# The last projection with w3 stationary and 512 tokens moving; x1 is turned instead of z2

## The chip, the cores and the metric

One core of one Trainium2 chip runs the whole program. The metric is the time of one execution on the device, in microseconds (us). TensorE is PE in the views, VectorE is DVE, ScalarE is ACT, GpSimd is POOL; SP is the engine that issues most DMAs, and its rows are "SPq".

## The reference

The input is 16 sequences of 256 tokens with 256 features. A first block adds to x a gated attention over a context (an mLSTM form with 8 heads), fed with the layer norm of x. A second block is the feed-forward part that this change touches:

```python
x = x + attention(layernorm(x), ctx)                # called x1 in the kernel
h = silu(lin(layernorm(x), w1, s1)) * lin(layernorm(x), w2, s2)   # 256 -> 1024
h = gelu(lin(h, h1, s)); h = gelu(lin(h, h2, s))    # 1024 -> 1024, twice
x = x + lin(h, w3, s3)                              # 1024 -> 256, scaled per output feature
```

The weights of the linear layers are ternary, each with one scale per output feature. layernorm(x1) is called z2.

## The kernel before, in words

The work is cut into 8 pairs of sequences, 512 tokens each. `batch(i, ...)` is written once for each engine and unrolled over i = 0 to 7. In batch i TensorE runs the feed-forward part of pair i, and between its matmuls stand the attention of pair j = i + 1 and the gates of pair g = i + 2. In batches 0 to 5 all three are there, batch 6 has no gates (`g_stage` is false), batch 7 only the feed-forward part.

Feed-forward values are held features by tokens: the partitions are 128 features, the 512 tokens are the free axis. Each value is split into two parts, a rounded `h_hi` (ACT) and the rest `h_lo` (DVE), and each product is two matmuls. A layer has 8 groups m of 128 output features; a group of a hidden layer is 16 matmuls with 512 moving columns. There are four steps in a batch: `swiglu` (64 matmuls), two `hidden_layer`s (128 matmuls each, the second is called layer 3 in the code's `after_3`), and `project`.

After each group of a hidden layer ACT applies the gelu and makes `h_hi` (`gelu`, L762 and L765), and DVE makes `h_lo` (`lo`, L1184). DVE's program is one fixed list: what stands between two `lo` calls delays the later one. `gelu` of group m waits for `lo` of group m - 4, since they share a buffer of four. `project` waits for `lo` of group k before it uses the values of group k, and for all groups' PSUM banks to be free.

The second norm of pair j lies in batch i = j - 1, around layer 3: DVE makes x1 in `xs` (`residual`), its moments (`norm_2_stats`), the inverse root (`norm_rsqrt`, 11 small instructions), and z2, tokens by features (`norm_2_apply`, L906). TensorE turns z2 into features by tokens (`turn_z2`, 8 transposes, L1356) right ahead of `project`; ACT and DVE split it into `z2_hi` and `z2_lo` (L744, L1165), for which the first matmul of the next batch waits (`s_z2lo`).

`project` of before has the hidden values stationary (128 features by 128 tokens) and 256 columns of w3 moving, so its result is tokens by features, like x1; `finish` scales it by w3's scales (L1196) and adds x1 (L1202).

The SP engine's list is in one order as well, and each DMA may wait for a semaphore, with all behind it waiting too. In batch 6 it writes x1 of pair 7 to DRAM (`keep_x1`, L439), and then issues `load_raw` for 10 blocks of the raw weights (L459). They go to `decay`, four slots in turn, and DVE's `compare` (L1235) looks at each block for a weight that the rounding changed. If there were one, a second path over all pairs would run from the x1 kept in DRAM; with these inputs that path is skipped. `compare` of blocks 0 to 5 stands on DVE behind `lo` of groups 2 to 7 of batch 6.

For the first norm of pairs 2 to 7 the kernel has another form already: the input is loaded features by tokens, and mean and inverse root are written to DRAM (`moment_rows`, L379), read back spread over all partitions into `z` (L381), and applied with two `tensor_tensor` operations (`norm_in_place`, L933 and L935).

## Time and profile before

| | |
|---|---|
| median of 3 runs | 759.57 us (757.95 to 759.61) |
| profiled execution | 757.76 us, its span 756.0 us |
| granted TensorE clock | 0.999 over the span |
| busy: PE, DVE, ACT, POOL | 745.9, 540.9, 366.2, 23.9 us |

The span runs from the first to the last instruction. A matmul's shown duration is longer than the distance to the next one's start, since matmuls are pipelined; the distances between starts are what TensorE pays. Times in the rows below are counted from the span's start.

### The profile page before, as it was taken

The numbers are of one execution on the slowest core, as the hardware profiler recorded it, in microseconds if no ns is written. First come the engines' busy times: TensorE is split into PE (matmuls) and PEld (weight loads), VectorE is DVE, ScalarE is ACT, GpSimd is POOL, SyncE is SP. The second block draws the span as 40 slices with busy tenths as digits, with TensorE's granted clock in tenths as the row PEclk, the third lists the DMA queues.
The fourth block names the chain that finished last, engine by engine and source line by source line (L and its number), as shares of the span: only waits on it lengthen the run. The fifth ranks groups of instructions, "written<-read, shape, count | busy, mean of one in ns | idle before, by whom it ended". The sixth has DMA issues, their size and how long they took to land.

```text
span 756.0 us, 15309 instructions
## 1 busy us (share of the span) xinstructions
PE 745.9 (99%) x6344; PEld 620.3 (82%) x6344; DVE 540.9 (72%) x1289; ACT 366.2 (48%) x559; POOL 23.9 (3%) x52
## 2 busy tenths in 40 slices
PE   8999999999999999999999999999999999999998
PEld 4778888888898888988888888888789888898887
DVE  6788686686957859587785869669595774965554
ACT  3566436463535625456364644556253562445332
POOL 3400000000000000000000000000000000000000
PEclk9999999999999999999999999999999999999999
DMA  8293213202022030411232031320202100540540
GB/s 335 83 406 145 62 62 138 84 28 87 34 113 84 29 87 35 151 45 33 86 125 101 1 92 58 113 85 28 87 34 113 56 1 3 194 140 27 168 140 31
DMA packets 19417, 70.38 MB, mean 93 GB/s; under 512 B 4128, under 2 KB 6160, under 8 KB 16528
## 3 DMA queue, kind: packets, MB, share of 16 engines
q1 hardware_dynamic: 17760, 57.03, 22.1%
q0 software_dynamic: 1296, 11.53, 3.9%
q8 instruction: 52, 0.85, 0.5%
q10 hardware_dynamic: 288, 0.79, 0.3%
q14 instruction: 21, 0.17, 0.1%
HBM read 60.42 MB, written 8.92 MB: 92 GB/s over the span
## 4 chain that ended last, share of the span: by engine, by line
PE 93%; DVE 1%; issue 0%; ACT 0%
PE ps_f L1605 31%; PE ps_f L1606 31%; PE ps_f L1570 8%; PE ps_f L1571 8%; PE ps_f L1645 4%; PE ps_f L1646 4%; PE ps_a L1510 2%; PE ps_a L1493 2%; PE ps_a L1543 1%; PE ps_a L1356 1%; PE ps_a L1466 1%; PE ps_a L1502 0%; PE ps_f L1580 0%; DVE stats L1078 0%; DVE z L1065 0%
## 5 line engine op out<-in xcount | busy, mean ns | idle before, releaser
L1605 PE MATMUL ps_f<-h_hi,wgt 128*128 128x512 f32 x1024 | 401.5, 392 | 0.0
L1606 PE MATMUL ps_f<-h_lo,wgt 128*128 128x512 f32 x1024 | 398.8, 389 | 0.0
L1605 PEld LDWEIGHTS ps_f<-h_hi,wgt 128*128 128x128 f32 x1024 | 192.2, 188 | 41.9 <-ACT work L762 1.2
L1606 PEld LDWEIGHTS ps_f<-h_lo,wgt 128*128 128x128 f32 x1024 | 192.3, 188 | 39.2
L762 ACT ACTIVATE work<-ps_f,scl 128x512 f32<-128x512 f32 x128 | 87.7, 686 | 221.3 <-PE ps_f L1606 221.1
L1184 DVE TENSOR_TENSOR h_lo<-work,h_hi 128x512 fp32r<-128x512 f32 x128 | 85.5, 688 | 91.2 <-ACT h_hi L765 90.3
L1570 PE MATMUL ps_f<-h_hi,wgt 128*128 128x512 f32 x252 | 99.2, 393 | 0.0
L1571 PE MATMUL ps_f<-h_lo,wgt 128*128 128x512 f32 x252 | 98.3, 390 | 0.0
L749 ACT ACTIVATE work<-ps_f,scl 128x512 f32<-128x512 f32 x64 | 44.2, 690 | 88.3 <-PE ps_f L1571 87.6
L765 ACT ACTIVATE h_hi<-work 128x512 fp32r<-128x512 f32 x128 | 81.0, 633 | 4.1
L1175 DVE SCALAR_TENSOR_TENSOR work<-ps_f,scl,work 128x512 f32<-128x512 f32 x64 | 48.1, 751 | 39.5 <-PE ps_f L1571 38.3
L1000 DVE SCALAR_TENSOR_TENSOR decay<-decay,cols,future 128x128 f32<-128x128 f32 x224 | 64.5, 364 | 0.0
L1645 PE MATMUL ps_f<-wgt,h_hi 128*128 128x256 f32 x256 | 62.4, 285 | 0.0
L1646 PE MATMUL ps_f<-wgt,h_lo 128*128 128x256 f32 x256 | 61.8, 283 | 0.0
L1570 PEld LDWEIGHTS ps_f<-h_hi,wgt 128*128 128x128 f32 x252 | 47.3, 188 | 10.6 <-DVE work L1175 0.4
L1571 PEld LDWEIGHTS ps_f<-h_lo,wgt 128*128 128x128 f32 x252 | 47.3, 188 | 9.4
L1646 PEld LDWEIGHTS ps_f<-wgt,h_lo 128*128 128x128 f32 x256 | 49.1, 192 | 0.0
L1645 PEld LDWEIGHTS ps_f<-wgt,h_hi 128*128 128x128 f32 x256 | 49.1, 192 | 0.1
L675 ACT ACTIVATE decay<-decay 128x1024 f32<-128x1024 f32 x28 | 29.7, 1061 | 35.3 <-DVE decay L1000 35.3
L1180 DVE TENSOR_TENSOR h_lo<-work,h_hi 128x512 fp32r<-128x512 f32 x64 | 43.7, 682 | 0.8
L753 ACT ACTIVATE h_hi<-work 128x512 fp32r<-128x512 f32 x64 | 39.9, 623 | 4.4 <-DVE work L1175 4.3
L1016 DVE SCALAR_TENSOR_TENSOR decay<-ps_a,decay 128x512 f32<-128x512 f32 x60 | 37.1, 678 | 1.1 <-PE ps_a L1493 1.1
(207 smaller groups left out, 596.2 us busy)
## 6 DMA issues: line engine op xcount, KB each, us to landing
decay<-m_rows SPq DMA_DIRECT2D x14, 1024.0 KB, 6.6
decay<-w_cols SPq DMA_DIRECT2D x22, 512.0 KB, 4.5
wgt<-w_cols POOLq DMA_DIRECT2D x5, 1024.0 KB, 11.6
v_aug<-ctx_tok SPq DMA_DIRECT2D x8, 528.0 KB, 5.0
wgt<-w_cols POOLq DMA_DIRECT2D x2, 2048.0 KB, 13.7
x_kept<-xs SPq DMA_DIRECT2D x8, 512.0 KB, 2.7
xs<-x SPq DMA_DIRECT2D x7, 512.0 KB, 3.6
ctxT<-ctx_t SPq DMA_DIRECT2D x7, 512.0 KB, 3.3
```

The costliest lines, as they stand in the source:

```text
L749: act.activation(work[:, m % 2], ps_f[:, bank], ACT.Silu, scale=scl[:, 0, m:m + 1]).then_inc(s_silu, 1)
L762: act.activation(work[:, m % GELU], ps_f[:, (turn_of(i) + m) % 4], ACT.Gelu, scale=scl[:, 2 + layer, m:m + 1]).then_inc(s_gelu, 1)
L765: act.activation(h_hi[1 - layer][:, m], work[:, m % GELU], ACT.Copy).then_inc(s_hi, 1)
L1000: last = dve.scalar_tensor_tensor(part, part, cols[:, t, row:row + 1], future[:], ALU.subtract, ALU.add)
L1175: dve.scalar_tensor_tensor(work[:, 2 + m % 2], ps_f[:, bank], scl[:, 1, m:m + 1], work[:, m % 2], ALU.mult, ALU.mult).then_inc(s_hf, 1)
L1184: dve.tensor_tensor(h_lo[1 - layer][:, m], work[:, m % GELU], h_hi[1 - layer][:, m].bitcast(F32), ALU.subtract).then_inc(s_lo, 1)
L1570: pe.matmul(ps_f[:, bank + half], w, moving(z2_hi[:, c], as_is), start=(c == 0), stop=False)
L1571: last = pe.matmul(ps_f[:, bank + half], w, moving(z2_lo[:, c], as_is), start=False, stop=(c == CH - 1))
L1605: pe.matmul(ps_f[:, bank], w, moving(h_hi[layer][:, k], as_is), start=(k == 0), stop=False)
L1606: last = pe.matmul(ps_f[:, bank], w, moving(h_lo[layer][:, k], as_is), start=False, stop=(k == KH - 1))
L1645: pe.matmul(to, moving(h_hi[0][:, k, q * P:(q + 1) * P], as_is), w, start=(k == 0), stop=False)
L1646: last = pe.matmul(to, moving(h_lo[0][:, k, q * P:(q + 1) * P], as_is), w, start=False, stop=(k == KH - 1))
```

## The change

- `project` has w3 stationary (128 hidden by 128 output features) and 512 tokens moving: 32 matmuls of 512 columns where 64 of 256 stood. The last pair's second half is cut in two pieces of 256 tokens. The result is features by tokens, so `finish` is one operation for each of two banks, with w3's scale per partition, and the output is written in that layout.
- x1 must be in that layout too. TensorE turns x1 (`turn_x1`) behind group 4 of layer 3, where it turned z2 behind group 7; ACT copies it from PSUM into `xs` (`take_x1T`) behind the gelu of group 4.
- The second norm is done on the turned x1: DVE's `norm_rsqrt` and two small copies of the moments (`keep_moments`) stand ahead of `lo` of group 0; SP sends the moments to DRAM and spreads them back (`spread_moments(1, ...)`); `norm_2_turned`, two `tensor_tensor` of 1024 columns, stands behind `lo` of group 5. `z2_hi` and `z2_lo` are made from SBUF.
- `keep_x1` waits for the turned x1, and z2 is kept in DRAM as well (`keep_z2`, 8 more DMAs of 512 KB). Pair 0 keeps its z2 in an extra ACT copy, and its x1 is turned in `swiglu`, behind m = 3.
- `compare` writes its marks into `zT` instead of `z`.

```diff
-            def spread_moments(j):
-
-                sp.wait_ge(s_moments, j - W + 1)
-                reuse(sp, s_moments_in, 16 * (j - W))
-                sp.dma_start(moment_rows.rearrange("k p q -> p k q"), moments[:]).then_inc(s_moments_out, 16)
-                sp.wait_ge(s_moments_out, 16 * (j - W) + 16)
+            def spread_moments(n, turn):
+
+                rows_out = moment_rows[n]
+                sp.wait_ge(s_moments[n], turn + 1)
+                reuse(sp, s_moments_in[n], 16 * turn)
+                sp.dma_start(rows_out.rearrange("k p q -> p k q"), moments[n][:]).then_inc(s_moments_out[n], 16)
+                sp.wait_ge(s_moments_out[n], 16 * turn + 16)
+                if n:
+                    sp.wait_ge(s_zTe, min(turn + 3, PAIRS))
                 sp.dma_start(z[:].rearrange("p q d -> p (q d)"),
-                             moment_rows.rearrange("(o k) p q -> o (k p q)", o=1).to_broadcast([P, 2 * NT])).then_inc(s_moments_in, 16)
+                             rows_out.rearrange("(o k) p q -> o (k p q)", o=1).to_broadcast([P, 2 * NT])).then_inc(s_moments_in[n], 16)
...
             def keep_x1(j):
-                sp.wait_ge(s_resid, RESIDUAL_STEPS * (j + 1))
-                sp.dma_start(x1_kept[j], xs[j % 2][:]).then_inc(s_x1kept, 16)
+                sp.wait_ge(s_x1T, j + 1)
+                sp.dma_start(x1_kept[j], resident_turned(j)).then_inc(s_x1kept, 16)
+
+            def keep_z2(j):
+                if first(j):
+                    sp.wait_ge(s_z2_taken, 1)
+                else:
+                    sp.wait_ge(s_z2, j)
+                sp.dma_start(z2_kept[j], z2_turned).then_inc(s_z2kept, 16)
...
+            keep_z2(0)
             keep_x1(0)
...
-                    spread_moments(g)
+                    spread_moments(0, g - W)
...
                 if j < PAIRS:
+                    spread_moments(1, j - 1)
                     keep_x1(j)
...
+                if j < PAIRS - 1:
+                    keep_z2(j)
                 if i == PAIRS - 2:
                     for n in range(COMPARED_BEFORE_LAST + RAW):
                         load_raw(n)
+                    keep_z2(j)
...
-                act.wait_ge(s_z2T, j + 1)
-                act.activation(z2_hi, ps_a[:, 0:CH], ACT.Copy).then_inc(s_z2hi, 1)
+                if isinstance(j, int):
+                    act.wait_ge(s_z2, j)
+                else:
+                    act.wait_ge(s_z2in, 16 * (j - PAIRS) + 16)
+                act.activation(z2_hi, z2_turned, ACT.Copy).then_inc(s_z2hi, 1)
+
+            def copy_first_z2():
+
+                act.activation(z2_turned, ps_a[:, 0:CH], ACT.Copy).then_inc(s_z2_taken, 1)
+
+            def take_x1T(j):
+                act.wait_ge(s_x1turn, j + 1)
+                if not first(j):
+
+                    act.wait_ge(s_norm2, NORM_STEPS * (j - 1) + 1)
+                act.activation(resident_turned(j), ps_a[:, 0:CH], ACT.Copy).then_inc(s_x1T, 1)
...
+                    if a_stage and m == 4:
+                        take_x1T(j)
...
+            def norm_2_turned(j):
+                dve.wait_ge(s_moments_in[1], 16 * (j - 1) + 16)
+                dve.wait_ge(s_x1T, j + 1)
+                dve.tensor_tensor(by_tile(z2_turned), by_tile(resident_turned(j)), moment_spread(0), ALU.subtract).then_inc(s_z2_centred, 1)
+                dve.wait_ge(s_z2_centred, j)
+                dve.tensor_tensor(by_tile(z2_turned), by_tile(z2_turned), moment_spread(1), ALU.mult).then_inc(s_z2, 1)
...
             def finish(i):
 
-                kept = resident(i)[:].rearrange("p (b t) d -> p b (t d)", b=W)
-                scale = w3s_b[:].rearrange("p (o d) -> p o d", o=1).to_broadcast([P, TILES, DIM])
+                kept = resident_turned(i)
                 if first(i):
                     dve.wait_ge(s_w3s, 16)
-                for b in range(W):
-                    dve.wait_ge(s_ymm, Q * i + W * TILES - W + b + 1)
-                    bank = (turn_of(i) + b) % 4
-                    dve.tensor_tensor(y_tmp[:, b].rearrange("p (t d) -> p t d", t=TILES),
-                                      ps_f[:, bank].rearrange("p (t d) -> p t d", t=TILES), scale, ALU.mult).then_inc(s_ysc, 1)
                 if isinstance(i, int):
                     dve.wait_ge(s_x1kept, 16 * i + 16)
-                for b in range(W):
-                    dve.wait_ge(s_ysc, W * i + b + 1)
-                    dve.tensor_tensor(kept[:, b], y_tmp[:, b], kept[:, b], ALU.add).then_inc(s_y, 1)
+                else:
+                    dve.wait_ge(s_x1in, 16 * (i - PAIRS) + 16)
+                for c in range(CH):
+                    dve.wait_ge(s_ymm, CH * i + c + 1)
+                    dve.scalar_tensor_tensor(kept[:, c], ps_f[:, (turn_of(i) + c) % 4], w3s[:, c:c + 1], kept[:, c],
+                                             ALU.mult, ALU.add).then_inc(s_y, 1)
...
                     norm_2_stats(j, xs[j % 2])
+                    norm_rsqrt(s_norm2, j)
+                    keep_moments(1, j - 1)
                 for m in range(KH):
                     lo(i, 1, m)
-                    if a_stage and m == 1:
-                        norm_rsqrt(s_norm2, j)
-                        norm_2_apply(j, xs[j % 2])
+                    if a_stage and m == 5:
+                        norm_2_turned(j)
                     if g_stage and m == 1:
...
-            def turn_z2(j):
-                pe.wait_ge(s_z2, j)
-                turn(z2, ps_a[:, 0:CH], s_z2T)
+            def turn_x1(j):
+                pe.wait_ge(s_resid, RESIDUAL_STEPS * (j + 1))
+                if first(j):
+                    pe.wait_ge(s_z2_taken, 1)
+                    pe.wait_ge(s_z2lo, 1)
+                turn(resident(j), ps_a[:, 0:CH], s_x1turn)
...
             def project(i, as_is, final):
                 per = UNIT // DIM
 
-                def part(b, t, ks):
-                    q = b * TILES + t
-
-                    n = q if final else b
-                    bank, col = (turn_of(i) + n) % 4, 0 if final else t * DIM
+                def part(c, n, at, ks):
+
                     for k in ks:
                         if as_is and k % per == 0:
                             pe.wait_ge(*unit_landed(i - PAIRS, UNIT_W3 + k // per))
 
                         pe.wait_ge(s_lo, 2 * KH * i + KH + max(k + 1, 5 + n))
-                        w = columns(UNIT_W3 + k // per, k % per * DIM, DIM, as_is)
-                        to = ps_f[:, bank, col:col + DIM]
-                        pe.matmul(to, moving(h_hi[0][:, k, q * P:(q + 1) * P], as_is), w, start=(k == 0), stop=False)
-                        last = pe.matmul(to, moving(h_lo[0][:, k, q * P:(q + 1) * P], as_is), w, start=False, stop=(k == KH - 1))
+                        w = columns(UNIT_W3 + k // per, k % per * DIM + c * P, P, as_is)
+                        to = ps_f[:, (turn_of(i) + n) % 4, at]
+                        pe.matmul(to, w, moving(h_hi[0][:, k, at], as_is), start=(k == 0), stop=False)
+                        last = pe.matmul(to, w, moving(h_lo[0][:, k, at], as_is), start=False, stop=(k == KH - 1))
                     return last
 
+                whole, left, right = slice(0, NT), slice(0, SEQ), slice(SEQ, NT)
                 if final:
-                    for t in range(TILES):
-                        part(0, t, range(KH - 1))
-                    for t in range(TILES):
-                        part(0, t, range(KH - 1, KH)).then_inc(s_ymm, 1)
+                    part(0, 0, whole, range(KH - 2))
+                    part(1, 1, left, range(KH - 2))
+                    part(0, 0, whole, range(KH - 2, KH)).then_inc(s_ymm, 1)
                     count_inexact()
-                    for t in range(TILES):
-                        part(1, t, range(KH)).then_inc(s_ymm, 1)
+                    part(1, 1, left, range(KH - 2, KH)).then_inc(s_tail_ymm, 1)
+                    part(1, 2, right, range(KH)).then_inc(s_ymm, 1)
                     return
-                for b in range(W):
-                    part(b, 0, range(KH - 1))
-                for b in range(W):
-                    part(b, 0, range(KH - 1, KH)).then_inc(s_ymm, 1)
-                for b in range(W):
-                    part(b, 1, range(KH)).then_inc(s_ymm, 1)
+                for c in range(CH):
+                    part(c, c, whole, range(KH - 2))
+                for c in range(CH):
+                    part(c, c, whole, range(KH - 2, KH)).then_inc(s_ymm, 1)
...
+                    if first(i) and m == 3:
+                        turn_x1(0)
...
-                    if a_stage and m == 7:
-                        turn_z2(j)
+                    if a_stage and m == 4:
+                        turn_x1(j)```

The lists of three engines show where this moves instructions. SP, around batch 6, before; `xs1` holds pair 7's x1, `w_cols` are the raw weights:

```order
L433 DMA decay<-m_rows 128x2048 x2
L443 DMA out<-xs1 128x1024
L399 DMA xs1<-x 128x1024
L439 DMA x1_kept<-xs1 128x1024
L459 DMA decay<-w_cols 128x1024 x10
L443 DMA out<-xs0 128x1024
```

And SP at the same place after the change:

```order
L413 DMA xs1<-x 128x1024
L391 DMA moment_rows1<-moments1 128x2x4
L395 DMA z<-moment_rows1 128x1024
L453 DMA x1_kept<-xs1 128x1024
L481 DMA decay<-w_cols 128x1024 x10
L460 DMA z2_kept<-num 128x1024
L464 DMA out<-xs0 128x1024
```

The ten weight blocks still stand behind the copy of x1, but that copy now stands behind two new DMAs and waits for the turned x1.

DVE in layer 3 of batch 6, before. L1184 is `lo`, L1235 is `compare`; the rows ahead of the piece are `lo` of groups 0 and 1 and the inverse root:

```order
L906 TENSOR_SCALAR num<-xs1,mv,nw 128x256 x4
L1184 TENSOR_TENSOR h_lo0<-work,h_hi0 128x512
L1235 SCALAR_TENSOR_TENSOR z,inexact<-decay,wgt 128x1024
L1184 TENSOR_TENSOR h_lo0<-work,h_hi0 128x512
L1235 SCALAR_TENSOR_TENSOR z,inexact<-decay,wgt 128x1024
L1184 TENSOR_TENSOR h_lo0<-work,h_hi0 128x512
```

DVE at that place after the change, from the end of the inverse root on; L1238 is `lo`, L1280 is `compare`, L993 and L995 are `norm_2_turned`:

```order
L976 COPY moments1<-mv 128x4
L977 COPY moments1<-nw 128x4
L1238 TENSOR_TENSOR h_lo0<-work,h_hi0 128x512 x3
L1280 SCALAR_TENSOR_TENSOR zT,inexact<-decay,wgt 128x1024
L1238 TENSOR_TENSOR h_lo0<-work,h_hi0 128x512
L1280 SCALAR_TENSOR_TENSOR zT,inexact<-decay,wgt 128x1024
L1238 TENSOR_TENSOR h_lo0<-work,h_hi0 128x512
L1280 SCALAR_TENSOR_TENSOR zT,inexact<-decay,wgt 128x1024
L1238 TENSOR_TENSOR h_lo0<-work,h_hi0 128x512
L993 TENSOR_TENSOR num<-xs1,z 128x1024
L995 TENSOR_TENSOR num<-num,z 128x1024
L1280 SCALAR_TENSOR_TENSOR zT,inexact<-decay,wgt 128x1024
```

The norm has moved from a place ahead of the first `compare` to one behind the third, and is two wide operations.

TensorE at the end of layer 3 of batch 6, before, with z2's eight transposes between the layer and the projection:

```order
L1605 MATMUL ps_f<-h_hi1,wgt 128x512
L1606 MATMUL ps_f<-h_lo1,wgt 128x512
L1356 MATMUL ps_a<-ident,num 128x128 x8
L1645 MATMUL ps_f<-wgt,h_hi0 128x256
L1646 MATMUL ps_f<-wgt,h_lo0 128x256
```

And TensorE behind group 4 of the same layer after the change, with x1's transposes among the layer's matmuls:

```order
L1651 MATMUL ps_f<-h_hi1,wgt 128x512
L1652 MATMUL ps_f<-h_lo1,wgt 128x512
L1398 MATMUL ps_a<-ident,xs1 128x128 x8
L1651 MATMUL ps_f<-h_hi1,wgt 128x512
L1652 MATMUL ps_f<-h_lo1,wgt 128x512
```

The transposes have moved three groups forward, and a second change of form inside the layer comes with them.

## Rows read from the trace of the kernel before

**Rows 1.** The page: busy time by engine, and shares of the last chain.

```profile
PE 745.9 (99%) x6344; PEld 620.3 (82%) x6344; DVE 540.9 (72%) x1289; ACT 366.2 (48%) x559; POOL 23.9 (3%) x52
...
PE 93%; DVE 1%; issue 0%; ACT 0%
```

**Rows 2.** Waits of TensorE: who was waited for, us in total, times, longest.

```profile
PE ps_a L1510 <- issue: 1.9, 1, 1.9
```

**Rows 3.** Timeline of TensorE, batch 6, layer end to next batch: start us, us.

```profile
659.52 0.39 PE L1605 MATMUL ps_f<-h_hi,wgt 128*128 128x512 f32 x1
...
663.15 1.03 PE L1356 MATMUL ps_a<-ident,num 128*128 128x128 f32 x8
663.94 0.36 PE L1645 MATMUL ps_f<-wgt,h_hi 128*128 128x256 f32 x1
...
671.69 0.40 PE L1570 MATMUL ps_f<-h_hi,wgt 128*128 128x512 f32 x1
```

**Rows 4.** Timeline of TensorE in batch 1, behind the gates and behind layer 3.

```profile
197.32 0.50 PE L1605 MATMUL ps_f<-h_hi,wgt 128*128 128x512 f32 x1
197.65 0.40 PE L1606 MATMUL ps_f<-h_lo,wgt 128*128 128x512 f32 x1
...
215.59 1.04 PE L1356 MATMUL ps_a<-ident,num 128*128 128x128 f32 x8
```

**Rows 5.** Timeline of DVE, the last instruction of the span.

```profile
752.88 0.42 DVE L1225 TENSOR_TENSOR xs<-num,xs 128x256 f32<-128x256 f32 x1
```

**Rows 6.** Groups of DVE: busy us, mean ns, then idle before.

```profile
L933 DVE TENSOR_TENSOR zT<-zT,z 128x1024 f32<-128x1024 f32 x6 | 12.0, 2000 | 18.5 <-DMA zT<-x_t 18.5
L935 DVE TENSOR_TENSOR zT<-zT,z 128x1024 f32<-128x1024 f32 x6 | 11.9, 1980 | 0.2
L926 DVE COPY moments<-mv 128x4 f32<-128x4 f32 x6 | 1.0, 170 | 0.2
```

**Rows 7.** DMA issues, median us to landing: the moments on their way out.

```profile
moment_rows<-moments SPq DMA_DIRECT2D x6, 4.0 KB, 2.1
```

**Rows 8.** Line L381, the spread of the moments.

```profile
DMA to landing us min/median/max: 3.7/4.0/5.0
```

**Rows 9.** Line L459, the loads of raw weight blocks.

```profile
DMA to landing us min/median/max: 3.5/4.5/6.6
```

**Rows 10.** Timeline of SP in batch 6.

```profile
647.63 0.34 SPq L439 DMA_DIRECT2D x_kept<-xs  x1
648.01 18.91 SPq L459 DMA_DIRECT2D decay<-w_cols  x10
```

**Rows 11.** Timeline of DVE in batch 6, layer 3.

```profile
649.69 1.29 DVE L1184 TENSOR_TENSOR h_lo<-work,h_hi 128x512 fp32r<-128x512 f32 x2
650.90 0.16 DVE L851 TENSOR_SCALAR nw<-nw 128x4 int32<-128x4 int32 x1
...
653.08 1.39 DVE L906 TENSOR_SCALAR num<-xs,mv,nw 128x256 f32<-128x256 f32 x4
...
655.11 1.22 DVE L1235 SCALAR_TENSOR_TENSOR z<-decay,wgt 128x1024 bf16<-128x1024 f32 x1
...
656.86 1.22 DVE L1235 SCALAR_TENSOR_TENSOR z<-decay,wgt 128x1024 bf16<-128x1024 f32 x1
...
666.49 1.22 DVE L1165 TENSOR_TENSOR h_lo<-ps_a,h_hi 128x1024 fp32r<-128x1024 f32 x1
```

**Rows 12.** Timeline of ACT in batch 6: gelu of group 4, and z2_hi.

```profile
652.47 0.69 ACT L762 ACTIVATE work<-ps_f,scl 128x512 f32<-128x512 f32 x1 [2.27 <-PE ps_f L1606]
...
664.61 1.01 ACT L744 ACTIVATE h_hi<-ps_a 128x1024 fp32r<-128x1024 f32 x1
```

**Rows 13.** Timeline of DVE in batch 1: lo of groups 0 and 1, and 7.

```profile
203.82 1.29 DVE L1184 TENSOR_TENSOR h_lo<-work,h_hi 128x512 fp32r<-128x512 f32 x2
...
217.18 0.69 DVE L1184 TENSOR_TENSOR h_lo<-work,h_hi 128x512 fp32r<-128x512 f32 x1 [2.63 <-ACT h_hi L765]
```

**Rows 14.** A stretch: us, busy of PE, PEld, DVE, ACT, POOL, clock, DMA share, GB/s.

```profile
528.00:536.00 8.00, 6.13 (x180) 5.01 (x179) 6.80 (x27) 3.16 (x5) 0.00 (x0) 1.00 0.03 3
```

143 lines of the change are left out of this document (75 added, 68 removed).

## The prediction

> **What bounds the kernel now.** I read the page first: TensorE is busy in 99% of the span and carries 93% of the chain that ended last, where DVE is busy in 72% and ACT in 48% [rows 1]. In the waits of TensorE one entry has more than a microsecond, 1.9 us once, released by nothing that the profile shows [rows 2]. So the time is the sum of what TensorE issues, and everything else costs only once it is late for TensorE. Then the timeline, for distances between starts: group 7 of layer 3 of batch 6 has 16 matmuls of 512 columns from 659.52 to 663.15, 0.227 us each; the turn of z2 takes 0.79 (663.15 to 663.94), and the 64 matmuls of 256 columns of the projection 7.75 (663.94 to 671.69), 0.121 each [rows 3]. Behind a change of form the first distance is longer: 0.33 where 0.227 is usual, behind the gates [rows 4], and I count 0.1 for it.
>
> **TensorE's own sum.** The projection becomes 32 matmuls of 512 columns: 32 x 0.227 = 7.26, with the first's 0.1 it is 7.4 against 7.75 [rows 3]. That is 0.4 less for each of pairs 0 to 6, 2.8 in all. The last pair has 16 wide and 32 narrow matmuls, 3.63 + 3.87 + 0.1 = 7.6, so 0.15 less. Together -2.95. The columns are the same; what is saved is a fixed part of each matmul (2 x 0.121 - 0.227 = 0.015 us).
>
> x1's turn costs what z2's did, but it stands alone among matmuls of another form, and in batches 0 to 5 the turn of the gate rows then stands alone too. Each such place costs a second first distance, 0.1, and perhaps as much again on entry: I take 0.15 for six batches, +0.9 (bounds 0 and 0.2 each). Pair 0 gets a turn that it did not have: 0.79 + 0.1 [rows 3, 4], so +0.9, with its ACT copies (1.0 each, as the copy of z2 [rows 12]) beside a SwiGLU in which ACT idles. At the end DVE's separate add of 0.42 [rows 5] is gone, since scale and add are one operation: -0.4. The sum of these is -2.95 + 0.9 + 0.9 - 0.4 = about -1.5 us.
>
> At the projection a rule speaks against this term. The Trainium skill, "TensorE: Matmul & The Clock Gate", Back-to-back issue gap, gives an isolated distance of N / 2.4 + 2.5 ns. By it 64 of 256 columns are 6.99 us and 32 of 512 are 6.91, a gain of 0.08 per pair, and as estimates from that page TensorE's sum would be +0.8 instead of -1.5. The rows have a fixed part six times as large, and the sum above goes by them.
>
> **DVE in the batches with gates (0 to 5).** Ahead of `lo` of group 0 now stand the inverse root, 653.08 - 650.90 = 2.2 [rows 11], and two copies (0.17 each, overlapping [rows 6]); counted 0.2. In batch 1 that puts the moments at 203.82 + 2.4 = 206.2 [rows 13]. The trip out takes 2.1 [rows 7] and with the issue I count 2.6; the spread takes 4.0 [rows 8]; so they are back at 212.8. DVE gets to that place at about the same time, since gelu of group 4 and the ACT copy of x1 stand before `lo` of group 5. `norm_2_turned` is of the form of L933 and L935, 2.00 + 1.98 [rows 6], not two of the 1.22 that a plain operation over 1024 columns takes [rows 11]: done at 216.8. `lo` of groups 6 and 7 follow by 218 (the last was at 217.18 before [rows 13]); z2_hi (1.0) and z2_lo (1.2) by 219.7. TensorE ends layer 3 of batch 1 at 215.6 [rows 4]; with the turns kept at 0.2 the projection starts at 215.8 and can run k = 0 to 5 of both halves, 24 x 0.227 = 5.4, before it asks for group 6, at 221.2, and the next batch asks for z2_lo at 223.1. Both have a slack of about 3.4 us. Cost nothing, if the trip of the moments is not 3.4 us later. DVE's saving at `finish` (two adds) lies beside TensorE's next SwiGLU and brings nothing.
>
> **Batch 6.** Here the cover is thin, because DVE also has six `compare` operations, and because of SP's order. Before, `keep_x1` was issued at 647.63, right behind the residual, the first raw block at 648.01 [rows 10], and DVE began the first `compare` at 655.11 with no wait for it [rows 11]. Now `keep_x1` waits for the turned x1, which waits for ACT, which waits for gelu of group 4, which waits for `lo` of group 0:
> - DVE: 649.69 + 2.4 = 652.1, `lo` of group 0 to 652.8; three `lo` end at 654.0.
> - ACT: gelu of group 4, before at 652.47 [rows 12], now at 652.8; gelu and h_hi 1.3, copy of x1 1.0, to 655.2.
> - SP: copy of x1 at 655.2, first raw block 0.4 later, at 655.6, that is 7.6 later than before. The spread of the moments (issued at 654.8, 512 KB) and the copy of x1 (512 KB) are ahead of it in the queue.
> - The block lands after a median of 4.5, between 3.5 and 6.6 [rows 9]. I take 4.8 for what is ahead of it: 660.4. DVE has stood still from 654.0.
>
> From there DVE's list is dense: `compare` and `lo` repeat every 1.75 (655.11 to 656.86 [rows 11]). Three of them end at 665.65, `norm_2_turned` (4.0) at 669.65, two more at 673.15, the last `compare` (1.15) at 674.3, z2_lo (1.2) at 675.5. z2_hi (1.0) is ready long before, at 670.7. TensorE: layer 3 ends at 663.15 + 0.79 + 0.1 = 664.05, and the projection would end at 671.3. It will halt for `lo` of group 6 (needed at 669.5, there at 671.4) and of group 7 (673.15), finish at 674.5, and then stand for z2_lo until 675.6. All three waits together are 675.6 - 671.3 = **4.3 us**, once.
>
> Bounds: with a landing of 3.5 it is 3.0, with 6.6 it is 6.1; if `norm_2_turned` takes two plain operations, 2.4 instead of 4.0, it is 1.6 less. So 1.4 to 6.1. The later blocks are needed 1.75 apart and transfer faster than that in the before. Without the wait for the first block the same list ends at 669.1, 2.2 ahead of need: the wait must be over 2.2 us to cost, and I have it at 6.4.
>
> **Sum.** -1.5 + 4.3 = +2.8 us. Against the profiled execution (span 756.0 and 1.8 around it, 757.76) that is 760.6. The median of the three runs is 759.57, 1.8 above that execution, and with it the sum gives 762.4. Runs of before lie at both, so I predict the middle, 761.5.
>
> **Rivals.**
> - *The raw blocks come in time, or DVE catches up* (13%). For it: DVE was ready early before, and the first block might be issued before the copy of x1 is asked for; against it SP's list, where it stands behind. Then TensorE's sum alone is left: -1.5, 756.3 by the profiled execution, 758.1 by the median. The change is then not slower; a wait for the block below 2.2 us decides.
> - *Same path, small stall* (6%). The norm takes 2.4 and the block lands early, 1.4 to 2 us in all: the net is about 0, 757.8 to 759.6.
> - *A stall in every batch with gates* (7%). If the moments or the ACT copy come over 3.4 us later than worked out, every further microsecond costs TensorE six times; 1 us over makes +6 on the forecast, 767. The spread took at most 5.0 instead of 4.0 [rows 8], so one slow trip doesn't do it.
> - *The clock* (4%). TensorE stood 1.9 us in the stretch 528 to 536 and was granted the full 2.4 GHz there, 1.00 [rows 14]. Three waits in a row in batch 6 could bring the level of 1.2 GHz; each microsecond of matmuls would then take two. 4 us of work at that level make +4, 765.5.
> - The rest, 70%, is the forecast.
>
> **Range and chances.** About 0.3% (2.3 us) is what a measurement of this kernel can tell from no change. The forecast's net runs from -0.1 to +4.6 by its bounds; its centre 2.8 is little over 2.3, and I give 48 of its 70 to over 2.3 and 22 to within. Slower: 48 + 7 + 4 = 59. Same: 22 + the small stall 6 + 7 of the first rival = 35. Faster: 6, the rest of the first rival, with a TensorE gain nearer 2.8. The range goes from 757.8, where no stall is on the median's level, to 764.5, the longest landing on that level.
>
> **What would show it.** In the profile after: distances in the projection of 0.227, and 7.4 us from its first matmul to the next batch (right or wrong for the gain); no idle time of TensorE at the boundaries of batches 0 to 5 (the slack); the two norm operations at 2.0 each; the first raw block issued near 655 less what was gained by then, DVE idle ahead of the first `compare` for some 6 us, released by a DMA, and TensorE idle about 4 us between 668 and 676 for DVE. The prediction is wrong if that idle time isn't there, or if one is there in every batch.

## The result, and the profile after

The changed kernel takes 765.01 us (median of 4 runs, 764.67 to 765.34), the kernel before beside it 759.57 (757.95 to 759.61): a ratio of 1.0075 (95% interval 1.0063 to 1.0088). It is slower, as predicted, and by 5.4 us where +1.9 was forecast (761.5, range to 764.5). Its profiled execution took 764.84 us with a span of 763.0.

The page of after, busy times and shares of the last chain:

```profile
PE 747.9 (98%) x6112; PEld 610.0 (80%) x6112; DVE 550.3 (72%) x1270; ACT 374.2 (49%) x568; POOL 23.8 (3%) x52
...
PE 11%; DVE 4%; DMA 1%; issue 1%; ACT 0%; SPq 0%; DVEq 0%; ACTq 0%
```

The waits of TensorE in after (who was waited for, us in total, times, longest):

```profile
PE ps_f L1688 <- DVE h_lo L1238: 3.6, 2, 3.2
PE ps_a L1556 <- issue: 2.9, 2, 1.9
...
PE ps_f L1616 <- DVE h_lo L1219: 0.7, 1, 0.7
```

Before, the one unreleased wait was 1.9 us, for nothing that the profile shows [rows 2]. Now there are two kinds of new waits: for DVE in the projection (L1688) and at the next SwiGLU (L1616), and a second of the unreleased ones. The chain, 93% TensorE before [rows 1], goes back through DVE and a DMA and is lost there, so its sum of shares is small; what matters is that DVE and a DMA (`decay<-w_cols`) now stand in it.

The first kind, from its end to its cause. The timeline of TensorE in batch 6 of after (start us, us, idle before and its releaser; compare [rows 3]):

```profile
664.17 0.39 PE L1652 MATMUL ps_f<-h_lo,wgt 128*128 128x512 f32 x1
667.77 0.76 PE L1688 MATMUL ps_f<-h_hi,wgt 128*128 128x512 f32 x1 [3.21 <-DVE h_lo L1238]
668.33 0.63 PE L1689 MATMUL ps_f<-h_lo,wgt 128*128 128x512 f32 x1
668.76 0.63 PE L1688 MATMUL ps_f<-h_hi,wgt 128*128 128x512 f32 x1
...
676.94 0.50 PE L1688 MATMUL ps_f<-h_hi,wgt 128*128 128x512 f32 x1 [0.41 <-DVE h_lo L1238]
...
679.32 0.47 PE L1616 MATMUL ps_f<-h_hi,wgt 128*128 128x512 f32 x1 [0.72 <-DVE h_lo L1219]
```

The timeline of DVE there (compare [rows 11]):

```profile
652.20 0.17 DVE L976 COPY moments<-mv 128x4 f32<-128x4 f32 x1
...
652.35 1.89 DVE L1238 TENSOR_TENSOR h_lo<-work,h_hi 128x512 fp32r<-128x512 f32 x3
664.04 1.23 DVE L1280 SCALAR_TENSOR_TENSOR zT<-decay,wgt 128x1024 bf16<-128x1024 f32 x1 [9.79 <-DMA decay<-w_cols]
...
669.29 2.03 DVE L993 TENSOR_TENSOR num<-xs,z 128x1024 f32<-128x1024 f32 x1
671.35 2.04 DVE L995 TENSOR_TENSOR num<-num,z 128x1024 f32<-128x1024 f32 x1
...
677.96 1.21 DVE L1219 TENSOR_TENSOR h_lo<-num,h_hi 128x1024 fp32r<-128x1024 f32 x1
```

And SP's list (compare [rows 10]):

```profile
652.47 0.38 SPq L391 DMA_DIRECT2D moment_rows<-moments  x1
655.01 0.32 SPq L395 DMA_DIRECT2D z<-moment_rows  x1
655.42 1.10 SPq L453 DMA_DIRECT2D x_kept<-xs  x1
656.57 21.82 SPq L481 DMA_DIRECT2D decay<-w_cols  x10
```

DVE stands still for 9.8 us until the first raw block is there, at 664.04, and from then on its list is dense: z2_lo ends at 679.17, 15.1 us later, and TensorE starts the next batch at 679.32. The blocks were issued at 656.57, 8.6 us later than before, behind the spread and the copy of x1.

The waits shown in batch 6 add up to only 4.3 us (3.6 + 0.7), yet the batch takes 95.18 us where it takes 87.51 without the late blocks (first experiment): 7.7 are lost. The rest hides in TensorE's busy time. The windows of after: us, busy of PE, PEld, DVE, ACT, POOL, clock, DMA share, GB/s.

```profile
664.00:668.00 4.00, 0.79 (x4) 0.40 (x3) 3.96 (x7) 1.32 (x2) 0.00 (x0) 0.82 0.70 229
668.00:672.00 4.00, 4.00 (x10) 3.13 (x11) 3.96 (x5) 0.00 (x0) 0.00 (x0) 0.50 0.79 256
672.00:676.00 4.00, 4.00 (x16) 3.21 (x16) 4.00 (x5) 2.35 (x2) 0.00 (x0) 0.83 0.23 48
```

Behind the 3.2 us of idle time the granted clock is 0.50, the level of 1.2 GHz, and the matmuls of the projection stand 0.43 apart instead of 0.227. That cost nothing by itself: DVE was busy in full beside it, and the end was z2_lo's. A wait of DVE's list turned partly into slow matmuls, and a sum of waits alone would have undercounted it. The first wait, 3.2 us, is at the start of the projection, for `lo` of group 4; the prediction had TensorE halt for group 6 first.

The second kind is new to the prediction. Times from the first SwiGLU matmul of one batch to the next, taken from TensorE's timeline (batch 0 from the span's start, the tail from the last matmul's start):

| us | 0 | 1 | 2 | 3 | 4 | 5 | 6 | 7 | tail |
|---|---|---|---|---|---|---|---|---|---|
| before | 134.97 | 89.35 | 89.35 | 89.35 | 89.35 | 91.39 | 87.93 | 80.41 | 3.94 |
| after | 135.65 | 88.95 | 90.14 | 91.11 | 89.32 | 88.95 | 95.18 | 80.33 | 3.40 |

Batches 2 to 4 of after are 1.2, 2.2 and 0.4 over the undisturbed 88.95, as batch 5 of before is 2.0 over 89.35. The two large ones in TensorE's timeline of after:

```profile
263.90 1.24 PE L1556 MATMUL ps_a<-v_aug,decay 128*32 128x33 f32 x117
266.08 0.32 PE L1556 MATMUL ps_a<-v_aug,decay 128*32 128x33 f32 x11 [0.94 <-issue]
...
354.04 1.32 PE L1556 MATMUL ps_a<-v_aug,decay 128*32 128x33 f32 x126
357.28 0.25 PE L1556 MATMUL ps_a<-v_aug,decay 128*32 128x33 f32 x2 [1.92 <-issue]
```

Both stand inside the 128 short matmuls of the attention's values, waiting for no semaphore. By the table the difference of the two spans, +7.0, is: TensorE's own sum -2.4 (0.4 less in each of batches 1 to 6, 0.7 more in batch 0, of which 0.2 stand ahead of its first SwiGLU matmul, 0.1 and 0.5 less in batch 7 and the tail), these waits +1.7 (3.7 against 2.0), batch 6's stall +7.7. The medians differ by less, 5.4, since the profiled execution of before lies 1.8 us under the median of its runs, and that of after 0.2 under its median. What sets the two levels of the kernel before is found below, under raw_early_moved.

### The profile page after: what moved, and what is told of

Its sections match the earlier page's. It is cut to its first block and busy times, and to the rows that moved or that the text cites. A ratio compares the mean times of both kernels' runs of the same rounds, so it can differ in the third digit from the quotient of the medians.

```text
span 763.0 us, 14886 instructions
## 1 busy us (share of the span) xinstructions
PE 747.9 (98%) x6112; PEld 610.0 (80%) x6112; DVE 550.3 (72%) x1270; ACT 374.2 (49%) x568; POOL 23.8 (3%) x52
## 5 line engine op out<-in xcount | busy, mean ns | idle before, releaser
L1651 PE MATMUL ps_f<-h_hi,wgt 128*128 128x512 f32 x1024 | 402.2, 393 | 0.2 <-issue 0.2
L1652 PE MATMUL ps_f<-h_lo,wgt 128*128 128x512 f32 x1024 | 398.8, 389 | 0.0
L1651 PEld LDWEIGHTS ps_f<-h_hi,wgt 128*128 128x128 f32 x1024 | 192.1, 188 | 41.7 <-ACT work L807 1.2
L1652 PEld LDWEIGHTS ps_f<-h_lo,wgt 128*128 128x128 f32 x1024 | 192.3, 188 | 39.4 <-issue 0.4
L1238 DVE TENSOR_TENSOR h_lo<-work,h_hi 128x512 fp32r<-128x512 f32 x128 | 85.9, 688 | 81.0 <-ACT h_hi L810 80.4
L1616 PE MATMUL ps_f<-h_hi,wgt 128*128 128x512 f32 x252 | 99.3, 394 | 0.7 <-DVE h_lo L1219 0.7
L1616 PEld LDWEIGHTS ps_f<-h_hi,wgt 128*128 128x128 f32 x252 | 47.3, 188 | 11.9 <-issue 1.1
L1688 PE MATMUL ps_f<-h_hi,wgt 128*128 128x512 f32 (+1 forms) x136 | 53.2, 396 | 3.6 <-DVE h_lo L1238 3.6
L1689 PE MATMUL ps_f<-h_lo,wgt 128*128 128x512 f32 (+1 forms) x136 | 52.1, 388 | 0.0
L1688 PEld LDWEIGHTS ps_f<-h_hi,wgt 128*128 128x128 f32 x136 | 26.5, 195 | 9.4 <-issue 3.6
L1280 DVE SCALAR_TENSOR_TENSOR zT<-decay,wgt 128x1024 bf16<-128x1024 f32 x22 | 26.8, 1217 | 9.8 <-DMA decay<-w_cols 9.8
```

Of the source, the lines that this page charges most:

```text
L1238: dve.tensor_tensor(h_lo[1 - layer][:, m], work[:, m % GELU], h_hi[1 - layer][:, m].bitcast(F32), ALU.subtract).then_inc(s_lo, 1)
L1616: pe.matmul(ps_f[:, bank + half], w, moving(z2_hi[:, c], as_is), start=(c == 0), stop=False)
L1651: pe.matmul(ps_f[:, bank], w, moving(h_hi[layer][:, k], as_is), start=(k == 0), stop=False)
L1652: last = pe.matmul(ps_f[:, bank], w, moving(h_lo[layer][:, k], as_is), start=False, stop=(k == KH - 1))
L1688: pe.matmul(to, w, moving(h_hi[0][:, k, at], as_is), start=(k == 0), stop=False)
L1689: last = pe.matmul(to, w, moving(h_lo[0][:, k, at], as_is), start=False, stop=(k == KH - 1))
```

## The experiments

The theory after the result: (T1) the late raw blocks hold DVE, and DVE holds TensorE in batch 6; the stall is the time of the first block plus 15.1 us of DVE's list. The rivals: DVE's list itself is too long (the norm behind `lo` of group 5); the wide projection doesn't gain; the copy of x1 alone is what delays the blocks. The kernel before was timed beside them: 759.25 us (26 runs) beside raw_early, no_compares, raw_ahead_of_copy and raw_early_narrow, 759.28 (17 runs) beside raw_mid, before_late, raw_early_shift and after_shift, 759.06 (13 runs) beside raw_early_moved and before_shift. Each ratio is to the kernel before of the same group.

### raw_early: the first four raw blocks ahead of the moments

```diff
+                if i == PAIRS - 2:
+                    for n in range(RAW):
+                        load_raw(n)
                 if j < PAIRS:
                     spread_moments(1, j - 1)
                     keep_x1(j)
...
-                    for n in range(COMPARED_BEFORE_LAST + RAW):
+                    for n in range(RAW, COMPARED_BEFORE_LAST + RAW):
                         load_raw(n)
```

> The changed kernel; in batch 6 SP issues the first four raw weight blocks ahead of the second norm's moments and of the copy of x1, all else as changed. Theory (the stall of batch 6 is the first block's late landing, 664.0, plus a dense DVE list of 15.1 us): DVE's first compare starts near 654 without a wait, TensorE has no wait at the end of batch 6, the granted clock stays at its full level, and batch 6 (start of one SwiGLU to the next) takes about 87.6 us instead of 95.2; time near 757.4, some 2 us under the kernel before. Rival (DVE's wide norm makes its list too long for batch 6 by itself): TensorE still waits for h_lo of groups 6 and 7, and the time stays over 760.

Measured: 758.55 us (11 runs), ratio 0.9992 (0.9983 to 1.0001). SP issues the blocks at 645.83, and DVE's first `compare` starts with no wait; its timeline in raw_early:

```profile
655.81 1.22 DVE L1283 SCALAR_TENSOR_TENSOR zT<-decay,wgt 128x1024 bf16<-128x1024 f32 x1
...
669.63 1.23 DVE L1222 TENSOR_TENSOR h_lo<-num,h_hi 128x1024 fp32r<-128x1024 f32 x1
```

z2_lo is done 2.4 us before TensorE asks for it at 673.29, and batch 6 takes 87.51 us, 0.42 less than before. The batch is 7.7 us shorter than in after, the kernel 6.5: the stall of batch 6 is the blocks' lateness and nothing else. That the time is 1.1 over the 757.4 expected has its cause in batches 2 to 4, found under raw_early_narrow. DVE's list with the norm behind group 5 isn't too long by itself.

### no_compares: blocks 0 to 5 aren't compared

```diff
-COMPARED_BEFORE_LAST = 6
+COMPARED_BEFORE_LAST = 0
+UNCOMPARED = 6
...
-                sp.dma_start(raw(n), w_cols[:, n * UNIT:(n + 1) * UNIT]).then_inc(s_raw[n % RAW], 16)
+                u = n + UNCOMPARED
+                sp.dma_start(raw(n), w_cols[:, u * UNIT:(u + 1) * UNIT]).then_inc(s_raw[n % RAW], 16)
...
```

It leaves out the look at six of the weight blocks (their marks are set to zero), so DVE has nothing in batch 6 that needs a DMA of SP's late list but the norm. The four blocks that SP still issues there are compared in batch 7.

> The changed kernel without the comparison of weight blocks 0 to 5 (that part of the check of the weights is left out): batch 6 has no compare, batch 7 its 16 as before; SP's order stays as changed, the raw blocks still behind the copy of x1. Theory (TensorE is late through DVE's wait for the first block): with no compare in front of h_lo the wait of batch 6 is gone, batch 6 takes about 87.6 us, time near 757.4 as with the blocks early. Rival (the turned x1, the trip of the moments or the norm itself arrive too late in batch 6): a wait of TensorE of some microseconds remains for z2_lo.

Measured: 758.51 us (10 runs), ratio 0.9988 (0.9978 to 0.9997), batch 6 again 87.51. Taking away the work that waits and taking away its wait give the same time within 0.1 us, so the six compares cost nothing where their data is there.

### raw_ahead_of_copy: four blocks ahead of keep_x1 alone

```diff
                     spread_moments(1, j - 1)
+                    if i == PAIRS - 2:
+                        sp.wait_ge(s_x1T, j + 1)
+                        for n in range(RAW):
+                            load_raw(n)
                     keep_x1(j)
```

> The changed kernel; in batch 6 SP waits for the turned x1 as changed, but issues four raw blocks ahead of the copy of x1 instead of behind it. Theory (the block is late by its issue, and by what is ahead of it in the queue: 1.1 us of issue and 512 KB, about 1.3 us of transfer): first block issued near 655.5 instead of 656.6, landing near 661 instead of 664.0, DVE's list 15.1 us from there to 676, TensorE's stall 4 to 5 us instead of 7.6; time near 762. Rival (the landing is late for another reason, such as the place of the block in the first burst): landing 7.4 us after issue again, near 663, time near 764.

Measured: 764.01 us (4 runs), ratio 1.0062 (1.0046 to 1.0077). SP's timeline in raw_ahead_of_copy, and DVE's:

```profile
658.15 2.89 SPq L481 DMA_DIRECT2D decay<-w_cols  x4
```

```profile
663.75 1.23 DVE L1284 SCALAR_TENSOR_TENSOR zT<-decay,wgt 128x1024 bf16<-128x1024 f32 x1 [6.93 <-DMA decay<-w_cols]
```

The blocks were issued at 658.15, and DVE began the first `compare` at 663.75, 5.6 us later, where it was 7.5 in after. The batch had begun 2.6 us later than in after (586.7 against 584.1, the sums of the periods), so against its own start the issue came 1.0 earlier and the landing 2.9. The batch takes 92.21, a stall of 4.7 us where after has 7.7. So the copy of x1 costs 3.0 us by these two profiles, in the issue and in the queue (1.4 against after_shift below, which has after's order of DMAs and a stall of 6.1); the wait for the trip of the moments and the turned x1, which the blocks still stand behind, costs the other 4.7. The rival of the copy alone falls. The stall is within the 4 to 5 us expected, the time is not (near 762): that it is only 1.0 us under after's has a cause outside batch 6, found below. Batches 2 to 4 are 1.8, 3.9 and 1.1 us over 88.95 here.

### raw_mid: four blocks right behind the moments, ahead of their trip

```diff
                 if j < PAIRS:
+                    if i == PAIRS - 2:
+                        sp.wait_ge(s_moments[1], j)
+                        for n in range(RAW):
+                            load_raw(n)
                     spread_moments(1, j - 1)
```

> The changed kernel; in batch 6 SP issues the first four raw blocks behind a wait for the moments of the second norm (near 652.5), ahead of their trip and of the copy of x1. Theory (dense list of 15.1 us from the first block's landing; TensorE asks for z2_lo 7.3 us behind the end of layer 3): landing near 657.3, z2_lo near 672.4 against a need near 671.8, a stall of 0.5 to 1 us in batch 6, where a stall of 7.6 was; the block's wait on DVE is over 3 us. Rival (any wait for a block costs in full): a stall of 3 us or more.

Measured: 763.74 us (4 runs), ratio 1.0064 (1.0048 to 1.008): a miss. SP's timeline in raw_mid, and DVE's:

```profile
653.75 1.76 SPq L481 DMA_DIRECT2D decay<-w_cols  x4
655.61 0.50 SPq L391 DMA_DIRECT2D moment_rows<-moments  x1
662.44 0.33 SPq L395 DMA_DIRECT2D z<-moment_rows  x1
```

```profile
657.50 1.23 DVE L1284 SCALAR_TENSOR_TENSOR zT<-decay,wgt 128x1024 bf16<-128x1024 f32 x1 [1.99 <-DMA decay<-w_cols]
...
667.56 1.98 DVE L997 TENSOR_TENSOR num<-xs,z 128x1024 f32<-128x1024 f32 x1 [4.71 <-DMA z<-moment_rows]
```

The blocks are there at 657.5, as wanted, but the 4 KB of moments, issued behind 2 MB of blocks, take 6.8 us where they take 2.1 alone [rows 7], and the spread waits for them. DVE now stands 4.7 us for the norm's data instead of for the blocks, and batch 6 takes 92.42. The Trainium skill, "DMA: Bandwidth & Descriptors", HWDGE ordering, says that on each DMA engine descriptors are consumed in the order of the ring; the 6.8 us agree. The stall is 4.9 us, as large as the rival had it, but not for the rival's reason: the wait for the block is only 2.0. So either of DVE's two inputs can make the stall, and here it was the one issued right behind the other's bytes. (In raw_early the moments were issued 8.3 us behind the first block, landed after 2.2 us, and nothing waited.)

### before_late: the kernel before, with its raw blocks issued late

```diff
                 if i == PAIRS - 2:
+                    sp.wait_ge(s_hi, 2 * KH * i + KH + 6)
                     for n in range(COMPARED_BEFORE_LAST + RAW):
                         load_raw(n)
```

> The kernel before, with SP holding the raw blocks of batch 6 until h_hi of group 5 of layer 3 (near 657.4 in its trace, 9.4 us later than it issues them). Theory (a late block suffices, the new norm isn't needed): the first block lands near 662, DVE's six compare and lo end at 672.5 and z2_lo at 673.7, against a need at 671.7: TensorE stands 1.5 to 2.5 us in batch 6, span 758, time 1.5 to 2.5 above the kernel before. Rival (late blocks are harmless without the norm in the list): no wait in batch 6 and the time of the kernel before.

Measured: 762.0 us (4 runs), ratio 1.0044 (1.0027 to 1.0062). The blocks are issued at 657.96, the first `compare` starts at 661.88 behind 6.2 us of idle time, z2_lo ends 11.1 us later at 673.0, and batch 6 takes 91.09, a stall of 3.2. Nothing of the change is in this kernel, and a late block alone makes the stall; it is over the 1.5 to 2.5 expected. z2_lo isn't late here: the next batch starts at 675.3, 2.3 us behind it. What holds TensorE is `lo` of group 6, done at 668.97, with 52 narrow matmuls of the projection still to be issued behind it; `lo` of group 7, done at 670.7, comes in time. The last wait in TensorE's timeline of before_late:

```profile
669.02 0.38 PE L1646 MATMUL ps_f<-wgt,h_hi 128*128 128x256 f32 x1 [1.25 <-DVE h_lo L1185]
```

In after the norm lengthens the list by 4.0, and, counted from the batch's start, the first block lands 2.3 us later still; there z2_lo is what ends last.

### raw_early_narrow: raw_early with the projection of pairs 0 to 6 in matmuls of 256 tokens

```diff
                 for c in range(CH):
-                    part(c, c, whole, range(KH - 2))
+                    part(c, c, left, range(KH - 2))
                 for c in range(CH):
-                    part(c, c, whole, range(KH - 2, KH)).then_inc(s_ymm, 1)
+                    part(c, c, left, range(KH - 2, KH))
+                for c in range(CH):
+                    part(c, c, right, range(KH)).then_inc(s_ymm, 1)
```

The edit of raw_early is in it as well. w3 stays stationary, but each matmul moves 256 tokens, so the projection has 64 of them again and the number of TensorE's instructions in a batch is that of before.

> As raw_early, but the projection of pairs 0 to 6 is 64 matmuls of 256 moving tokens with w3 stationary, in place of 32 of 512. Theory (the gain of the new projection is the fixed part of each matmul, 0.015 us, and nothing comes from which side is stationary): 7.75 us from the projection's first matmul to the next batch instead of 7.37, 0.4 more for each of seven pairs, time 2.7 us above raw_early. Rival (the stationary side matters): it stays within 1 us of raw_early.

Measured: 756.79 us (10 runs), ratio 0.9973 (0.9964 to 0.9983): 1.8 us *faster* than raw_early, where 2.7 slower was expected. The projection does take 7.75 instead of 7.37 in batches 0 to 5, and 7.67 instead of 7.25 in batch 6; but raw_early's table of batches reads 88.94, 90.43, 92.81, 89.5, 88.94 for batches 1 to 5, and narrow's 89.35, 89.35, 89.35, 89.99, 89.35. The wide form has 64 instructions fewer a batch (32 matmuls and their 32 weight loads). It gains 0.4 a batch and brings 5.9 us in batches 2 to 4, waits and one stretch at the lower clock. In raw_early's timeline of TensorE and its windows:

```profile
354.11 1.04 PE L1559 MATMUL ps_a<-v_aug,decay 128*32 128x33 f32 x95
357.15 0.25 PE L1559 MATMUL ps_a<-v_aug,decay 128*32 128x33 f32 x2 [2.01 <-issue]
```

```profile
354.00:358.00 4.00, 1.99 (x132) 1.74 (x122) 3.08 (x14) 1.53 (x3) 0.00 (x0) 1.00 0.06 5
358.00:362.00 4.00, 4.00 (x12) 3.12 (x11) 0.00 (x0) 0.05 (x1) 0.00 (x0) 0.57 0.49 134
```

A second theory, (T2): the waits come from the position of TensorE's instruction stream. The page of after has a queue of its own for it:

```profile
q8 instruction: 49, 0.80, 0.4%
```

That is 16 KB a packet (0.80 MB in 49). A batch has 1583 matmuls, weight loads and the like before and 1519 after. By the Trainium skill, "Runtime: NRT & Kernel Launch", Instruction fetch mechanics, the stream comes in blocks of 16 KB, 256 instructions, and crossing from one to the next is mostly hidden. The packets of 16 KB agree; that the crossing is hidden does not hold at the places below. 1583 is 47 over a multiple of 256 and 1519 17 under one, so the place of the border in a batch moves on by as much each batch. Counting TensorE's instructions from its first one, the short matmuls (320 instructions: 32 and 128 matmuls, each with a weight load) begin at these positions modulo 256; in bold where the wait stands:

| | 0 | 1 | 2 | 3 | 4 | 5 | 6 |
|---|---|---|---|---|---|---|---|
| before | 167 | 214 | 5 | 52 | 99 | **146** | 193 |
| after, raw_early | 184 | 167 | **150** | **133** | (116) | 99 | 82 |
| raw_early_narrow | 184 | 231 | 22 | 69 | (116) | 163 | 210 |

In after the waits fall behind 117 and 126 of the 128 (rows above), in before behind 119: 150 + 64 + 234 = 448, 133 + 64 + 252 = 449, 146 + 64 + 238 = 448. 64 are the first 32 matmuls with their loads, 234 twice 117. All three are the same place of a block. (116: the place lies just behind the short ones, and the batch is 0.4 to 1.1 us longer.)

The trace has the packets of this queue too. In after one of them runs from 354.90 to 355.96, inside the wait of 355.36 to 357.28; over 354.8 to 356.0 it is the only DMA of the core:

```profile
q8 instruction: 1, 0.02, 5.5%
```

The other wait of after (265.13 to 266.07) has its packet at 263.75 to 264.70, the wait of before (532.95 to 534.82) at 532.47 to 533.54. Each wait ends 1.3 to 1.4 us after the end of such a packet. The next four kernels try to move it.

### raw_early_shift and after_shift: 22 tiny products ahead of the first batch

```diff
+            def fill(products):
+
+                for _ in range(products):
+                    pe.matmul(ps_f[0:1, 3, 0:1], ones[:], ones[:], start=True, stop=True)
...
+            fill(22)
             pe.wait_ge(s_scan, 3)
```

Each product is two matmuls and two weight loads, so TensorE's stream is 88 instructions further along; the results are used by nobody. raw_early_shift is raw_early with this edit, after_shift is after with it.

> As raw_early, with 22 one-column products more on TensorE near the program's start (88 more instructions of its stream, where it waits for DVE anyway). In the trace of raw_early TensorE stands 1.5, 2.2 and 0.6 us in batches 2, 3 and 4 inside or right behind the short matmuls of the attention's values, each time while a 16 KB block of instructions is fetched. Counted from the start of that burst, the stream stands at instruction 184, 167, 150, 133, 116, 99, 82 modulo 256 in batches 0 to 6 of the changed kernel, and the stalls are at 150, 133 and 116. Theory (the stall depends on where a block of 256 instructions ends within the burst): 88 more instructions move all seven places out of 105 to 155, the three stalls are gone, span near 751.5 and time near 753.5, 5 us under raw_early. Rival (the stalls come from DMA traffic or another cause at these times): they stay, and the time is that of raw_early or a little more.

> The changed kernel with the same 22 products and nothing else. Theory: the stalls for instructions (3.7 us in the trace of the changed kernel, 2.0 in that of the kernel before) go, the stall of batch 6 stays at some 7.5 us; time near 760.5 to 761. Rival: no change from 765.

Measured: raw_early_shift **753.93 us** (6 runs, 753.34 to 754.6), ratio 0.9933 (0.992 to 0.9946), and after_shift 760.33 (10 runs), ratio 1.0021 (1.0011 to 1.0031). The waits of TensorE in raw_early_shift no longer have an unreleased one:

```profile
PE ps_f L1774 <- POOL ident L624: 2.1, 1, 2.1
PE ps_a L1487 <- DVE num L1148: 0.7, 1, 0.7
PE ps_a L1464 <- DVE num L1105: 0.4, 1, 0.4
```

Both take some 4.6 us less than without the products, by doing more work. after_shift keeps a stall in batch 6 (93.6 us): 6.1 where after has 7.7, since its first block is there 6.5 us from its issue instead of 7.5, and the issue comes 0.7 earlier in the batch. raw_early_shift is faster than the kernel before by 0.67%, than after by some 1.4%, and is the version to take.

### raw_early_moved and before_shift: is it the position?

The 22 products could help in another way than by position. raw_early_moved is raw_early with `fill(55)`, 220 instructions; before_shift is the kernel before with `fill(22)`.

> raw_early_shift with 55 instead of 22 tiny products ahead of the first batch, so TensorE's stream is 220 instructions further along than in raw_early. If the waits of TensorE that nothing releases come from where the stream's blocks of 256 instructions end within the short matmuls of a batch, they are now in batches 0 to 2 (near 87, 176 and 265 us, 1 to 2.2 us each, about 4 in all) and none is left in batches 3 to 5 (near 355 and 449 us), and the time is that of raw_early plus the filling, 758 to 759.5. If the 22 products removed the waits in another way (a later start, other DMA traffic), 55 of them leave the waits away too, and the time is 754 to 755.

> The kernel before, with the 22 tiny products of raw_early_shift ahead of the first batch. By the theory of the stream's blocks its one wait of 2.07 us without a releaser moves from batch 5 (532.7 us) to batch 3 (near 355 us), and the time stays within 0.5 us of before, 759 to 760. If the 22 products help by themselves, the wait is gone and the time is some 2 us less, 757.5.

Measured: before_shift 759.9 us (10 runs), ratio 1.0009 (0.9998 to 1.0021). Its wait has moved from batch 5 to batch 3, as worked out; TensorE's timeline of before_shift:

```profile
353.12 1.29 PE L1510 MATMUL ps_a<-v_aug,decay 128*32 128x33 f32 x122
356.57 0.26 PE L1510 MATMUL ps_a<-v_aug,decay 128*32 128x33 f32 x6 [2.17 <-issue]
```

raw_early_moved: its waits are in batches 0 and 1, with a small one in batch 2 (0.6), and none behind; its timeline:

```profile
88.19 1.25 PE L1559 MATMUL ps_a<-v_aug,decay 128*32 128x33 f32 x118
91.60 0.28 PE L1559 MATMUL ps_a<-v_aug,decay 128*32 128x33 f32 x10 [2.15 <-issue]
...
179.51 1.32 PE L1559 MATMUL ps_a<-v_aug,decay 128*32 128x33 f32 x127
182.62 0.22 PE L1559 MATMUL ps_a<-v_aug,decay 128*32 128x33 f32 x1 [1.78 <-issue]
```

With starts at 140 in before_shift, and 148 and 131 in raw_early_moved, the waits stand at 140 + 64 + 244 = 448, 148 + 64 + 236 = 448 and 131 + 64 + 254 = 449 again. So the position is shown, in six places and four programs, and in each of the six the wait ends 1.3 to 1.4 us after the end of an instruction packet.

The time of raw_early_moved is a miss: 764.35 is the median of its runs (760.51 to 766.39, 4 runs; 1.008, 1.0054 to 1.0106), and even the profiled execution, the shortest with 760.51 and a span of 758.7, is over the 758 to 759.5 expected. Its first SwiGLU matmul starts 2.7 us later than in raw_early, so the longer filling is not free. What the other three runs had more is in their clocks: 1.000 in the shortest, 0.995 in the one of 763.93, 0.993 in those of 764.77 and 766.39.

The same holds for the kernel before. In the 19 of its 56 runs with a clock of 0.999 or 1.000 over the span it took 757.5 to 758.8 us, in the 37 with 0.997 or 0.998 it took 758.8 to 760.4; the medians are 757.95 and 759.49. No profile of before itself has the lower clock, but that of before_shift has (0.997), behind its one long wait. The windows of before_shift, columns as above:

```profile
356.00:360.00 4.00, 3.43 (x16) 2.78 (x16) 0.71 (x2) 0.61 (x1) 0.00 (x0) 0.76 0.26 67
360.00:364.00 4.00, 4.00 (x16) 3.17 (x16) 0.28 (x1) 1.32 (x2) 0.00 (x0) 0.82 0.20 70
```

Shares of 0.76 and 0.82 are 3.4 us at the level of 0.50, some 1.7 us lost as an estimate, and over the span they make 0.998, near the 0.997 of that run. All 16 runs of raw_early_narrow and raw_early_shift, which have no wait of over 0.5 us at such a place, have 0.999 or 1.000. So one long wait for the stream costs its 2 us, and in some runs 1.7 more. That this is what parts the runs of before is argued from their clocks. Why the clock fell in one run and not in the other is open: in profiled executions it fell behind waits of 1.85, 2.0, 2.1 and 2.2 us, and not behind others of 1.9 and 2.15.

## Why the prediction was right or wrong

The step that failed is the time from the issue of the first raw block to its landing: 4.8 us were counted, 7.5 went by until `compare` started. The details, term by term:

- **TensorE's own sum, -1.5: too small a gain, -2.4 measured.** The projection was right: 7.37 us against 7.76, distances of 0.227, in each of pairs 0 to 5. The wrong term is the split of the turns, "0.15 for six batches, +0.9": a batch with both turns split takes 88.95, just 0.40 less than 89.35, so the split costs 0. Pair 0's batch, counted from its first SwiGLU matmul (88.02 before, 88.51 after), rose by 0.49 with the projection's -0.39 in it, so its turn costs 0.9, as predicted; the tail fell by 0.54 (0.4).
- **The norm in batches 0 to 5: right.** The operations took 2.0 each (2.03 and 2.04 in batch 6), and TensorE waits at no boundary of these batches; z2_lo is done 3.5 us ahead of need in each, where a slack of 3.4 was worked out. The rival of a stall in every batch with gates fell out. Batches 1 and 5, at 88.95, show it clean.
- **Batch 6, a stall of 4.3: right in mechanism, too small; 7.7 measured.** The dense list from the first `compare` to the end of z2_lo was worked out as 15.1 us and took 15.1; pricing the norm by L933 and L935 rather than by a plain operation was what made it right. The mis-sized term is when the first block lands: predicted 655.6 + 4.8 = 660.4, measured 656.57 and 664.04. Of the 3.6 us, 0.4 are a batch that began later (584.13 against 583.77), 0.6 the issue within it (SP took 1.10 to issue x1's copy, where I counted 0.4), and 2.7 the landing, 7.3 us from the issue and outside the 3.5 to 6.6 of [rows 9], with 0.1 more until `compare` starts. The spread, the copy and four blocks were asked for within a few microseconds, and the runs show what each adds: the first block lands after 3.8 us with neither just ahead of it (before_late; 3.6 in raw_mid), 5.5 behind the spread (raw_ahead_of_copy), 7.3 behind spread and copy (after; 6.4 in after_shift). Line L481 of after, over all its blocks:

```profile
DMA to landing us min/median/max: 3.4/4.5/9.0
```

  The longest landing of before, from a less crowded queue, was no bound.
- **The clock: the rival came true without a price.** 0.50 was granted behind a wait of 3.2 us, but inside the stall. As a price of its own it shows in raw_early, some 1.7 us in batch 3, and it fits the two levels that the prediction saw in the runs of before and averaged over, 757.76 and 759.57.
- **No term at all: where TensorE's stream is cut.** It gave +1.7 in the spans. I had read the 1.9 us of [rows 2] as "released by nothing that the profile shows" and left it there; it was the one number of before that the change, which takes 64 instructions out of each batch, was bound to move, and I carried it over as fixed. (The view that [rows 2] comes from has another wait of over a microsecond, 2.1 us for GpSimd at the program's start, which the prediction passed over; it is 2.1 in after as well.)

The sum by the measured terms is -2.4 + 1.7 + 7.7 = +7.0 of the spans, where -1.5 + 0 + 4.3 = +2.8 was predicted. The direction followed from the right chain and not from luck: without the +1.7 of the stream it would still be +5.3. The size lay outside the range since the landing's bound was the longest that before had, and the cut of the stream had no bound. The range itself is not quite what its terms give: -1.5 and +4.6 on 759.57 are 758.1 and 764.2, where 757.8 and 764.5 stand; 765.0 is outside either.

## What to carry to other kernels

When an early transfer is put behind a later event in one engine's list of DMAs, everything behind it moves as well: follow the list to the last one, and ask for each what starts only when it lands. Here one call moved ahead of the moments gave back 6.5 us. Order the small trip that others wait for ahead of bulk in the same queue, and bulk that is needed soonest ahead of what waits for a late event. Where TensorE is busy in 99% of the time, look at its unreleased waits inside runs of short matmuls, compare their position modulo 256 instructions, and try shifting the stream with a few idle products (22 helped here, 55 brought the waits back in other batches); any change of the number of instructions shifts it too, so a gain or loss of 2 to 6 us can come from nothing but that. Read the clock of every run beside its time, since a run at the lower level behind such a wait is longer again.
